# A fused LoRA FFN on one core: the down product's loads on GpSimd's queue, a third buffer for natural weights, and a new order of splits and tiles

## The reference, cut to what matters

```python
# layer 0, "cond": LoRA on gate, up and down; one expert for each of 32 sequences
gate = x @ W_gate.T + 0.5 * (x @ A_gate[e].T) @ B_gate[e].T     # 1376 columns
up   = x @ W_up.T   + 0.5 * (x @ A_up[e].T)   @ B_up[e].T
act  = silu(gate) * up
y    = act @ W_down.T + 0.5 * (act @ A_down[e].T) @ B_down[e].T
# layer 0, "ffn": an effective 512 x 512 matrix out of three low-rank parts
W_eff = (U_top * relu(S_top*alpha+beta)) @ Vh_top + (U_tail*S_tail) @ Vh_tail + delta
x1 = x + y @ W_eff.T + bias
# layer 1: language LoRA mixture on x1, RMS norm, and a gate/up/down FFN whose
# weights and activations are rounded to 8-bit steps (max over a row / 127)
```

## Time and profile before

| what | us |
|---|---|
| median of 3 runs (lowest, highest) | 421.41 (415.10, 423.12) |
| the profiled execution | 419.39 |
| span from its first to its last instruction | 417.6 |
| granted TensorE clock, mean | 0.974 |
| PE, DVE, ACT, POOL busy | 381.7, 279.0, 210.3, 110.0 |

### The profile page before, as it was taken

How to read it: one execution, slowest core, us unless ns; L and a number is a source line. 1 busy time by engine, 2 the same in 40 slices (tenths; PEclk the granted TensorE clock), 3 DMA queues, 4 the chain that set the end, 5 groups by cost and what they waited for, 6 DMA issues and landing times.

```text
span 417.6 us, 5954 instructions
## 1 busy us (share of the span) xinstructions
PE 381.7 (91%) x2098; PEld 318.6 (76%) x2101; DVE 279.0 (67%) x537; ACT 210.3 (50%) x349; POOL 110.0 (26%) x110
## 2 busy tenths in 40 slices
PE   8899998999999999999869787775899999999994
PEld 4598987999999999988869676664788887444442
DVE  5759647576486357645857658464358588989994
ACT  4616427354426345521748185383356554577671
POOL 3764543426440200100003000000000012556762
PEclk9889999999999999999998999968999999999999
DMA  8995491856845727340787949897055932122622
GB/s 282 359 336 169 134 343 55 246 176 187 286 119 145 244 81 232 115 183 27 214 213 225 257 105 255 204 342 246 11 180 120 217 119 47 39 54 76 96 85 102
DMA packets 68892, 72.31 MB, mean 173 GB/s; under 512 B 35249, under 2 KB 49099, under 8 KB 68735
## 3 DMA queue, kind: packets, MB, share of 16 engines
q1 hardware_dynamic: 53127, 54.88, 44.6%
q0 software_dynamic: 3488, 10.49, 8.1%
q10 hardware_dynamic: 12248, 6.56, 5.8%
HBM read 56.69 MB, written 7.75 MB: 154 GB/s over the span
## 4 chain that ended last, share of the span: by engine, by line
PE 55%; DVE 15%; DMA 12%; ACT 7%; SPq 6%; issue 3%; ACTq 2%; POOL 0%; DVEq 0%
PE ps L1460 19%; PE ps L1512 9%; PE ps L1535 5%; PE ps L1623 5%; DMA a_f<-act_scratch 5%; PE ps L1492 2%; DMA wg_raw<-w_gu_dram 2%; DVE hqs L1364 2%; DVE g_sb L1355 2%; DVE u_sb L1358 2%; ACT nat L768 2%; ACTq L691 2%; PE ps L1698 2%; PE ps L1446 2%; DMA act_scratch<-act_s 2%
## 5 line engine op out<-in xcount | busy, mean ns | idle before, releaser
L1460 PE MATMUL ps<-wg_hl,x_hl 128*128 128x352 f32 (+1 forms) x768 | 135.6, 326 | 5.6 <-DVE wg_hl L1015 2.1
L1460 PEld LDWEIGHTS ps<-wg_hl,x_hl 128*128 128x128 f32 x768 | 125.7, 193 | 11.2 <-issue 5.3
L1512 PE MATMUL ps<-act_hl,wd_hl 128*128 128x512 f32 (+1 forms) x264 | 66.9, 404 | 1.6 <-DVE wd_hl L1015 1.6
L1512 PEld LDWEIGHTS ps<-act_hl,wd_hl 128*128 128x128 f32 (+1 forms) x264 | 50.4, 197 | 11.7 <-DVE wd_hl L1015 1.9
L542 POOL DMA_INDIRECT b_raw<-b_gu_dram,idx_b x16 | 15.3, 958 | 128.0 <-DVE b_hl L1015 127.1
L739 ACT ACTIVATE sil<-ps 128x352 f32<-128x352 f32 (+1 forms) x32 | 14.6, 457 | 56.4 <-PE ps L1471 55.2
L588 POOL TENSOR_TENSOR qs<-qs,half 128x1 f32<-128x1 f32 x8 | 4.4, 550 | 121.6 <-DVE qs L1328 121.6
L1015 DVE TENSOR_TENSOR wg_hl<-wg_raw,wg_hl 128x704 fp32r<-128x704 f32 (+1 forms) x32 | 26.3, 863 | 13.0 <-ACT wg_hl L624 13.0
L1492 PE MATMUL ps<-act_hl,ad_hl 128*128 128x256 f32 (+1 forms) x132 | 21.0, 298 | 13.0 <-DVE act_hl L1015 13.0
L624 ACT ACTIVATE b_hl<-b_raw 64x704 fp32r<-64x704 f32 (+1 forms) x32 | 24.8, 774 | 14.2 <-PE ps L1471 7.4
L1015 DVE TENSOR_TENSOR b_hl<-b_raw,b_hl 64x704 fp32r<-64x704 f32 (+1 forms) x32 | 27.8, 870 | 5.8 <-ACT b_hl L624 4.8
(11 more groups left out here) (174 smaller groups left out, 656.2 us busy)
## 6 DMA issues: line engine op xcount, KB each, us to landing
wg_raw<-w_gu_dram SPq DMA_DIRECT2D x32, 352.0 KB, 3.7
wd_raw<-w_d_dram SPq DMA_DIRECT2D x22, 256.0 KB, 4.5
nat<-w_nat_dram SPq DMA_DIRECT2D x11, 512.0 KB, 4.0
a_f<-act_scratch SPq DMA_DIRECT2D x20, 256.0 KB, 4.5
act_scratch<-act_s ACTq DMA_DIRECT2D x24, 176.0 KB, 5.0
wdx<-w_nat_dram SPq DMA_DIRECT2D x11, 256.0 KB, 3.9
natd<-wd_nat_dram SPq DMA_DIRECT2D x4, 704.0 KB, 4.8
vu_raw<-w_vu_dram SPq DMA_DIRECT2D x3, 512.0 KB, 10.7
```

What stands on the lines that cost most here:

```text
L1460: mm(bank[:, 0:w], x_hl[n][:, v, k, t * P:(t + 1) * P], wg_hl[gu][:, u, k, 0:w], start=(k == 0 and (v, u) == THREE[0]), stop=False)
L1512: last = mm(ps[m][:], wd_hl[0:rows, slot, w, m * P:(m + 1) * P], act_hl[0:rows, slot, v, :], start=(f == 0 and (w, v) == THREE[0]), stop=F ...
```

## The change

1. **Down loads.** `load_wd`, `load_act` and `load_down` move from SP to POOL, between the gathers. POOL's list by chunk j: `load_down(done[0])`, `gather_b(2j+2)`, at j = 1 eight `agu` gathers, `load_down(done[1])`, at j = 3 eight `ad_raw` gathers, `gather_b(2j+3)`, at j = 3 eight more, then `load_down(done[2])`, where `done` is `downs_of(j - 1)`.
2. **Natural weights.** `nat` gets a third buffer, and SP's list becomes wdx(f+1), nat(f+3), turn(f) for each f.
3. **Splits in two parts.** `down_split` becomes `down_weights` (`ad_hl`) and `down_act` (`wd_hl`, `act_hl`), and both stand in other places in ACT's and DVE's lists. `wq_scale(f)` stands ahead of `silu(s)`, `wq_round(f)` behind it.
4. **Order of the first and last tiles.** `W_eff`'s part 2 is made ahead of step 0, the gate of step 1 is accumulated in bank TD, `delta` and the four `we_hl` splits come later, `down(0)` and `down(1)` move one step back, and in the last chunk `down(15)`, `down(16)`, `down(17)` and `down(18)` stand one step later.

```diff
-VU_SLOT = (0, 1, 1, 0)
+VU_SLOT = (0, 1, 0, 1)
+NATS = 3
...
+    nat = [sb(f"nat{i}", [P, 2 * H], fp32, at=at) for i, at in enumerate((D0 + 4096, D0 + 8192, NAT2))]
...
             load_vu(1)
+            load_vu(2)
...
             with sp.Fori(0, AGU_SP) as b:
                 load_a("a_gu", agu, b, agu_hw)
+            load_vu(3)
...
             def next_nat(f):
-                turn(f - 2)
-                load_nat(f)
-                load_wdx(f)
+                load_wdx(f + 1)
+                load_nat(f + NATS)
+                turn(f)
...
+            next_nat(0)
+            for i in range(2):
                 load_w(NCH + 3, i)
+            next_nat(1)
+            for i in range(2, 4):
+                load_w(NCH + 3, i)
+            for f in range(2, 8):
+                next_nat(f)
...
+            for j in range(1, CHUNKS):
+                done = downs_of(j - 1)
+                load_down(done[0])
+                if 2 * j + 2 < STEPS // 2:
+                    gather_b(2 * j + 2)
+                if j == 1:
+                    for b in range(8, 16):
                         gather_a("a_gu", agu, b, HB + b, agu_in[1])
+                load_down(done[1])
+                if j == 3:
                     gp.wait_ge(ag_made, 2 * NT)
+                    for b in range(0, 8):
                         gather_a("a_d", ad_raw, HB + b, HB + b, ad_in[1])
+                if 2 * j + 3 < STEPS // 2:
+                    gather_b(2 * j + 3)
+                if j == 3:
+                    for b in range(8, 16):
+                        gather_a("a_d", ad_raw, HB + b, HB + b, ad_in[1])
+                if j == NCH:
                     gather_bd(0)
+                if len(done) == 3:
+                    load_down(done[2])
...
+            def first_three(j, f=None):          # ACT; DVE's has the same order
+                d, s = downs_of(j - 1) if j else None, NT * j
+                for t in range(3):
+                    if s + t:
+                        b_split(s + t + 1)
+                        if t == 0 and j >= 2 and len(downs_of(j - 2)) == 3:
+                            down_act(downs_of(j - 2)[2])
+                        if t == 2 and j >= 2:
+                            down_act(d[0])
+                        if f is not None:
+                            wq_scale(f + t)
+                        silu(s + t)
+                        if f is not None:
+                            wq_round(f + t)
+                    if t and j >= 2:
+                        down_weights(d[t - 1])
...
+            gate_up(28)
+            gate_up(29)
+            down(15)
+            gate_up(30)
+            gate_up(31)
+            down(16)
+            down(17)
+            down(18)
```

More of the change, by code:

```diff
@@ L295, in build @@
         b_in = [sem("b_in0"), sem("b_in1")]
[L296 removed]
+        nat_in = [sem(f"nat_in{i}") for i in range(NATS)]
         wdx_in = sem("wdx_in")
@@ L386, in _ @@
                 load_w(1, i)
-            for d in range(2):
-                load_wd(d)
             with sp.Fori(0, AD_SP) as b:
@@ new lines, in last_one @@
+            def last_one(j, f=None):
+                d, s = downs_of(j - 1) if j else None, NT * j + 3
+                if j + 1 < CHUNKS:
+                    b_split(s + 1)
+                if j:
+                    down_act(d[1] if j >= 2 else d[0])
+                if f is not None:
+                    wq_scale(f)
+                silu(s)
+                if j + 1 < CHUNKS:
+                    refill(j + 1)
+                if f is not None:
+                    wq_round(f)
+            silu(0)
@@ L802, in _ @@
+            first_three(0)
+            last_one(0)
+            write_act(0)
+            b_split(5)
+            silu(4)
             for i in range(KT):
@@ L804, in _ @@
                 copy(we_hl[:, HI, i, :], ps[i][:]).then_inc(we_hi, 1)
-            for s in range(0, 6):
-                step(s)
+            b_split(6)
+            silu(5)
             act.wait_ge(vu_lo, WCH)
@@ L828, in _ @@
                 x1_split(q)
-            wq_round(0)
-            for s in range(24, STEPS):
-                step(s)
-                wq_scale(s - 23)
-                wq_round(s - 23)
+            first_three(NCH + 2, 1)
+            last_one(NCH + 2, 4)
+            write_act(NCH + 2)
+            down_weights(15)
+            b_split(29)
+            down_act(15)
+            wq_scale(5)
+            silu(28)
+            wq_round(5)
+            b_split(30)
+            wq_scale(6)
+            silu(29)
+            wq_round(6)
+            down_weights(16)
+            b_split(31)
+            wq_scale(7)
+            silu(30)
+            wq_round(7)
+            down_act(16)
+            down_weights(17)
+            silu(31)
+            down_act(17)
+            write_act(CHUNKS - 1)
+            down_weights(18)
+            down_act(18)
+            wq_scale(8)
+            wq_round(8)
             bd_split(1)
-            wq_scale(FT - 2)
-            wq_round(FT - 2)
             act.wait_ge(wc_in, 16)
@@ L1203, in _ @@
                 lo(x_hl[1][:, LO, pair(i)], x_raw[1][:, pair(i)], x_hl[1][:, HI, pair(i)]).then_inc(x_lo, 1)
-            for s in range(6, 10):
-                step(s)
-            ag_copy(1)
-            for s in range(10, 15):
-                step(s)
-            tg_mask(1)
-            for s in range(15, 20):
-                step(s)
+            b_split(7)
+            make_turn(6)
+            down_weights(0)
+            last_one(1)
+            down_weights(1)
+            down_act(1)
@@ L1212, in _ @@
+            for j in range(2, NCH + 1):
+                first_three(j)
+                if j == 2:
+                    ag_copy(1)
+                if j == NCH - 1:
+                    tg_mask(1)
+                last_one(j)
+                if j == NCH - 1:
+                    tg_low(1)
+                if len(downs_of(j - 1)) == 3:
+                    down_weights(downs_of(j - 1)[2])
             bd_split(0)
-            step(20)
+            b_split(21)
+            down_act(10)
+            make_turn(20)
@@ L1227, in _ @@
-            turn_act(23)
-            w_split(NCH + 2, 1)
+            last_one(NCH + 1)
+            wq_max(1)
             for q in range(KT):
                 x1_low(q)
-            wq_max(1)
-            for s in range(24, STEPS):
-                step(s)
-                wq_max(s - 22)
+            first_three(NCH + 2, 2)
+            last_one(NCH + 2)
+            wq_max(5)
+            down_weights(15)
+            b_split(29)
+            down_act(15)
+            make_turn(28)
+            wq_max(6)
```

373 lines of the change are left out of this document (203 added, 170 removed).

## The result

The changed kernel is slower: 428.25 us (median of four runs, 425.89 to 429.52) against 420.53 us before, a ratio of 1.025 with a 95% interval from 1.013 to 1.038. The forecast was 417 us with a range up to 426. In a later comparison the same kernel took 426.94 us, a ratio of 1.017 (1.011 to 1.022). Both intervals lie above 1; whether the loss is over 2% they leave open. The profiled execution took 429.5 us, its span 427.7 us, 10.1 us more than that of before.

A forecast was written before the change was run, and what follows sets the result against it. PE bound the kernel from 66 to 205 us, waits held it from 205 to 301 us. The span 417.6 - 1.5 (start) + 9 (part 7) - 10 (late stretch) + 1.8 around it gave 417 us, range 406 to 426.

The forecast's parts named there:

- the start: Up to part 0: less idle and half clock before 49 us, late splits at step 6; net about -1.5 us.
- the tail: From 301 us on: nothing that the change touches moves, so no gain or loss.
- part 7: Chunks 1 to 4: its loads on POOL come late behind 22 issues, stall 6.6 plus half clock 2.4, +9 us.
- the late stretch: After 205 us: down loads no longer wait behind transposes; 18 of 28 us still lost, so about -10 us.
- Step 6's wait: At the start: PE's step 6 waits about 2 us for splits on DVE behind turn_act(4) and the four we_hl subtractions.
- My sign against this step: Part 7: a POOL issue under 0.6 us would prove the +9 us step wrong; plain loads were priced at 1.25.
- The other chunks are hidden: Chunks 1 to 4 besides part 7: two or three loads and two gathers hidden by some 24 us of PE work.
- step 25 and the tiles: Late stretch: losses left after the change, 2.6 us at step 25 and 7 us for the tiles.
- the end of chunk 7: Late stretch: its write and a_f(19) come late, 4 us, and part 21 behind tile 10, 2: 6 us lost.
- the price of a tile: Late stretch: two tiles under way at a time, 6.2 us each; four steps without a down part lose 1.8 each.
- the slower rival: Late stretch: wq_scale ahead of silu ties PE to wdx, tiles cost 7.8, 13 us more, 430 us; chance 0.14.
- The rival that only issue time is saved: Late stretch: crowded transfers made the loads slow, so the late gain is only 3, 424 us; chance 0.11.

The follow-up runs named there:

- with part 7 in time: Changed kernel with the 44 down loads back on SP's queue, where silu 17 to 24 took 68.6 us: 422.79 us, ratio 1.007 to the kernel before.
- the queue alone: Kernel before with only the 44 down loads moved to GpSimd's queue, in the changed kernel's order: 437.43 us, ratio 1.050.
- the two kernels with 44 added ones: Kernel before plus 44 never-read loads on GpSimd's queue, of 128 rows in one and 16 in the other: spans 421.6 and 423.0 us.

## Why the prediction was wrong, point by point

Two steps failed: the price of the start, and the tail, which was put at nothing. A third place, part 10, was put at nothing too and cost less. The two large terms, part 7 and the late stretch, held.

- **The start (-1.5; measured +5.4, on the mean +2.2).** The gain up to step 2, put at 2.8 us, was 1 on the mean, and the loss behind it, put at 1.3 (I kept 1.5 of the gain), was 3.2. Step 6's wait was not what I had wrong: it was 3.36 us in the first profile, 0.87 in the second and 2.3 on the mean of the seven executions with this order, for 2 in the sum. What I had put at nothing stands around it. `delta`, 1.08 us, moved from a place where it covered a part of the wait for `tg_hl` (in the changed kernel PE stands 2.24 us for it, at 35.33) into a full stretch; I named the move and gave it no price. Part 1 waits 0.6 to 1.5 us in all seven. And behind the three longest waits at step 6, 3.2 to 3.4 us, the next base product ran at half clock and took 1.0 to 1.4 us more (the row at 66.30). That `down(0)` no longer waits held in three of the seven profiles; in the others it waits 0.7 us, where the kernel before had 1.64.
- **Part 7 (+9; measured +7.9).** Right in place and cause. The 22 issues took 26.0 us, from 112.83 to 138.81, where I had 27.5; the landing 7.4 instead of 4.5; the idle 5.6 instead of 6.6, the half clock 1.9 instead of 2.4. A plain load took 0.54 to 0.60 us of GpSimd and a gather mostly 1.25, so my price for plain loads was twice too high, and the landing made up for it: that the sum came so near is in part luck. My sign against this step, an issue under 0.6 us, was a wrong sign: it came, and the step held, since 18 of the 22 issues are gathers. The estimate from the fit of the Trainium skill (DMA: Bandwidth & Descriptors, section Anatomy of one DMA), 2.6 us for such a load, is below both medians of the changed kernel, 3.7 and 5.4.
- **"The other chunks are hidden" (0; measured +1.7, and 3.4 with part 7 in time).** Right of the queue, wrong of the change: part 10's splits got a new place behind `bd`'s, and I had not followed the new order there.
- **The late stretch (-10; measured -8.5, on the mean -7.6).** Right in sign and near in size. PE's idle time is 14.6 us, where I had about 16: 11.0 for silus (the sum had 9.6 for step 25 and the tiles) and 3.0 at the end of chunk 7 (the sum had 6). No down part of chunk 6 waits for `a_f`. But the price of a tile was wrong. The reductions of `wdx` came 5.6 to 13.4 us apart, and five of the eleven name its DMA; between the third and the ninth, 231.62 to 276.68, a tile took 7.5 us and not 6.2. By the slower rival the gain should be gone at 7.5. It was not, as that rival charged eight tiles and the sum only the four steps without a down part: PE stood 6.2 us and 3.4 us for two silus and under 1 us for two more. (A step's 28 matmuls at 0.168 us are 4.7 us and not 4.5; the timeline has 4.48, so nothing hangs on it.) The rival that only issue time is saved had its point: the queue alone gave about 4 us of the 7.6, by taking the loads out of a list with waits and transposes in it, and the runs do not split this further. The Trainium skill (DMA: Bandwidth & Descriptors, section Issuing engines are not separate DMA queues) says that another queue saves just the time to issue.
- **The tail ("From 301 us on nothing that the change touches moves"; measured +3.6).** The failed step that no row pointed to. I had read the tail up to its last instruction; the 0.9 us between the last landing and the span's end in the kernel before was all that could be seen of 5.8 us behind GpSimd's last instruction, and these grow with each DMA moved there.

The profiled execution lies 12.6 us above the forecast: 6.9 from the start, 3.6 from the tail, 1.7 from part 10, 1.5 from the late stretch, less 1.1 at part 7. Some 3 of the 6.9 are scatter; without them the time is about 426.5, at the range's edge. The range was too narrow because the terms put at nothing, the tail, part 10 and what surrounds step 6, could only add.

## What to carry to other kernels

When loads move to another engine's queue, list everything that queue issues in order and give each load the time of what stands ahead of it; here that foretold the one stall of 7.9 us. Move only the loads that profit: those of the late half, not those that had been in time. Read the time behind the last instruction as well, and follow a moved instruction to the new neighbours it gets, for a product that moves out of a place where its engine would wait anyway costs its full length. And profile the same kernel more than once before you explain a difference of 2 us: step 6's stall was 3.36 us in one execution and 0.87 in another.

## What the runs showed of the hardware

Each DMA added to GpSimd's queue cost 82 ns behind GpSimd's last instruction, whatever its rows and bytes: 5.8, 7.6 and 9.4 us for 67, 89 and 111. All that were added are plain loads, so the price of a gather there is not shown. The last output landed 4.9 us (before) and 3.6 us (changed) behind that instruction, so here the time lies open from 67 DMAs on. A plain load held GpSimd for 0.48 to 0.61 us, the 512-byte and 4 KB loads of the two kernels with 44 added ones as well as those of 256 KB, and the next followed at once; a gather mostly 0.94 with 0.30 behind it.
